# Where the zero fills of the sorted edge rows are issued in stage 1 of a graph network kernel

## The reference

```
def sage(x, W_l, b_l, W_r):
    agg = segment_sum(x[src], dst) / max(count(dst), 1)
    return agg @ W_l + b_l + x @ W_r
h = relu(sage(x, W_l1, b_l1, W_r1))
h = relu(sage(h, W_l2, b_l2, W_r2))
x = layernorm(x + h @ W_out + b_out)
# second network, per edge and then per node; row = src, col = dst
e = selu(concat(x[row], edge_attr) @ W1a + b1a) @ W1b + b1b
m = segment_sum(e, col) / max(count(col), 1)
y = selu(concat(x, m, u) @ W2a + b2a) @ W2b + b2b
out = layernorm(x + y)
```

## Time and profile before

| what | value |
|---|---|
| median of 3 runs | 2623.2 us (2621.38 to 2623.36) |
| the profiled execution's own time | 2619.25 us |
| its span | 2617.5 us |
| PE busy | 2105.8 us, 80% of the span |
| POOL busy | 1825.9 us, 70% |
| DVE busy | 1550.0 us, 59% |
| ACT busy | 987.8 us, 38% |
| fills of `sorted_edges` | 11 transfers of 1716 KB from SP's queue |

### The profile page before, as it was taken

The page is one execution under the profiler, slowest core; times in us unless marked ns, Lnnn a source line. Parts: engine busy times, 40 slices in busy tenths (PEclk is TensorE's granted clock), DMA queues, the critical chain, the costliest instruction groups (busy, mean ns, idle before and its releaser), DMA issues. The chain is left out here.

```text
span 2617.5 us, 52040 instructions
## 1 busy us (share of the span) xinstructions
PE 2105.8 (80%) x18382; PEld 1548.8 (59%) x18382; DVE 1550.0 (59%) x3098; ACT 987.8 (38%) x2255; POOL 1825.9 (70%) x1853
## 2 busy tenths in 40 slices
PE   1899999999999999847778787777787877866753
PEld 1555555555555555536666666666666666666753
DVE  6889999994455555545555555555555555543433
ACT  3777777771000000033333333333333333332322
POOL 5536766645766777677777777777777777777775
PEclk9989999999999999957898888988979889886555
DMA  8375787788677878334333333333333333322212
GB/s 293 126 230 191 208 257 225 202 250 227 231 231 226 240 232 239 86 103 115 74 72 69 72 68 68 75 68 71 74 63 78 72 62 79 68 61 51 54 40 45
DMA packets 478493, 346.45 MB, mean 132 GB/s; under 512 B 358165, under 2 KB 429008, under 8 KB 474574
## 3 DMA queue, kind: packets, MB, share of 16 engines
q1 hardware_dynamic: 367763, 272.49, 36.6%
q0 software_dynamic: 54240, 57.23, 9.9%
q10 hardware_dynamic: 56250, 13.52, 2.6%
HBM read 200.58 MB, written 142.39 MB: 131 GB/s over the span
## 5 line engine op out<-in xcount | busy, mean ns | idle before, releaser
L985 POOL DMA_INDIRECT A_sb<-source_terms,src_cur x1172 | 1120.3, 956 | 357.4 <-issue 351.6
L936 POOL DMA_INDIRECT sorted_edges<-pm_row,pm_to x440 | 482.2, 1096 | 171.1 <-issue 122.0
L1866 DVE TENSOR_TENSOR arena<-iota_code,arena 128x2048 f16<-128x2048 f16 (+1 forms) x392 | 438.5, 1188 | 33.7 <-PE cnt_ps L1413 31.3
L1080 ACT ACTIVATE A_sb<-cnt_ps 128x392 f32 (+1 forms) x784 | 384.1, 499 | 126.5 <-PE cnt_ps L1413 83.9
L1542 PE MATMUL agg_ps<-A_sb,arena 128*128 128x448 f16 x1911 | 375.5, 353 | 0.0
L2183 DVE TENSOR_TENSOR cnt_ps<-cnt_ps,A_sb 128x512 f32<-128x512 f32 x147 | 102.1, 695 | 459.3 <-DMA A_sb<-source_terms,src_cur 454.1
L1642 PE MATMUL agg_ps<-A_sb 128*65 128x48 f32 x2344 | 195.5, 245 | 181.4 <-DVE A_sb L2196 181.4
L1226 ACT ACTIVATE A_sb<-cnt_ps 128x512 f32<-128x512 f32 x147 | 87.6, 596 | 671.0 <-DVE cnt_ps L2183 665.7
L1413 PEld LDWEIGHTS cnt_ps<-arena 128*128 128x128 f16 x3136 | 190.2, 100 | 214.4 <-issue 168.8
L1413 PE MATMUL cnt_ps<-arena 128*128 128x98 f16 x3136 | 281.0, 214 | 31.3 <-ACT A_sb L1080 26.1
L1642 PEld LDWEIGHTS agg_ps<-A_sb 128*65 128x65 f32 x2344 | 181.2, 160 | 203.8 <-DVE A_sb L2196 198.6
(11 more groups left out here) (308 smaller groups left out, 3311.7 us busy)
## 6 DMA issues: line engine op xcount, KB each, us to landing
counts_matrix<-A_sb SPq DMA_DIRECT2D x14, 5488.0 KB, 17.4
A_sb<-counts_matrix SPq DMA_DIRECT2D x12, 5488.0 KB, 18.4
arena<-in_edge_attr_dram SPq DMA_DIRECT2D x96, 256.0 KB, 2.8
sorted_edges<-zrow SPq DMA_DIRECT2D x11, 1716.0 KB
A_sb<-source_terms,src_cur POOLq DMA_INDIRECT x1172
arena<-sorted_edges SPq DMA_DIRECT2D x143, 128.0 KB
overlapping_rows<-A_sb SPq DMA_DIRECT2D x1, 13056.0 KB, 39.3
A_sb<-in_edge_attr_dram SPq DMA_DIRECT2D x50, 256.0 KB, 2.8
```

The lines of the kernel that those rows point to most:

```text
L936: pool.indirect_dma_start(out=sorted_d, out_offset=bass.IndirectOffsetOnAxis(ap=pm_to[:, k, j:j + 1], axis=0), in_=pm_row[:, k, j, :], in_ ...
L985: pool.indirect_dma_start(out=gath[k][:, j * F:(j + 1) * F], out_offset=None, in_=p_d, in_offset=bass.IndirectOffsetOnAxis(ap=src_cur[k][: ...
L1080: act.activation(Asb(half)[:, :, bass.ds((b * BG + k) * GROUP, GROUP)].rearrange("p b (w j) -> p b w j", j=PAIR), cnt_ps[k % 2][:, 0:SUB * ...
L1866: ins = dve.tensor_tensor(hot_rows[:, slots], iota_code[:, 0:n, :].unsqueeze(1).to_broadcast([P, AT_ONCE * SUB // 2, n, 2]), turned[:, bas ...
```

## The change

Fills 0 to 10 are all issued inside `superblock(s)`, one per superblock from s = 2 to 12, behind the loads of group s-2 and ahead of the wait for the superblock's counts. Before, fills 0 and 1 were issued together between superblocks 1 and 2, and fills 2 to 10 behind the counts' stores of superblocks 4 to 12. The wait for scatter(0) stays ahead of fill 2 and moves with it. POOL's waits for the fills are not changed.

```diff
@@ -603,6 +603,10 @@
                 if s >= 2:
                     store_h(s - 2, half)
                     load_group(s - 2)
+                    if s == FIRST_SORT + 1:
+                        sp.wait_ge(pm_gone[0], 16 * EJ)
+                    if s - 2 < NR:
+                        blank(s - 2)
                 if s == NSB - 1:
                     for q in range(s - 1, IN_STAGE1 + PRING):
                         load_group(q)
@@ -619,15 +623,8 @@
                 sp.dma_start(pm_dst[:, :], dst[0:PG * EG].rearrange("(r q) -> r q", q=RG * EG)[:, 0].partition_broadcast(P)).then_inc(pm_dst_in, 16)
             superblock(0, 0)
             superblock(1, 1)
-            for r in range(2):
-                blank(r)
             for s in range(2, NSB):
                 superblock(s, s % 2)
-                if s >= FIRST_SORT + 1:
-                    if s == FIRST_SORT + 1:
-                        sp.wait_ge(pm_gone[0], 16 * EJ)
-                    if s - FIRST_SORT + 1 < NR:
-                        blank(s - FIRST_SORT + 1)
             sp.wait_ge(xT_ready, NSB - 2)
 
             def last_rows(rows, done):
```

## The result

The changed kernel takes 2613.15 us in the median of 8 runs (2611.82 to 2616.91), the kernel before 2621.51 us over 8 runs (2615.19 to 2623.85). The ratio is 0.9974 with a 95% interval of 0.9963 to 0.9985: 0.26% faster (the two medians alone lie 8.4 us, 0.32%, apart). Forecast were 2614.9 us and 0.32%. The profiled execution's span went from 2617.5 to 2611.2 us, 6.3 us less.

What follows compares the result with a forecast made beforehand. PE was taken to pace stage 1, losing time to a wait for x's rows held up by two fills, and its clock. -8.3 + 0 + 0 + 0 from 2623.2 gave 2614.9 us; range 2611.5 to 2620.5.

Steps and rivals of the forecast that it cites:

- The wait and its clock: Superblock 2, stage 1: PE's 2.93 us wait for x's rows and the clock's fall behind it go, gaining 8.3 us.
- The bottom-up sum: Superblock 2: 2.93 us of PE's wait plus 5.07 us of lowered clock make 8.0 us.
- rival 2: Superblock 2: only the wait goes, the clock's fall not coming from it; 2.9 us gained, 2620.3 us; chance 6%.
- Fills 2 to 10: SP's queue, superblocks 4 to 12: moving them from behind the counts' store to behind the group's load costs 0.
- The scatter beside a fill: POOL's scatter(s-3) issued beside a fill: no row; from below 0 to 8 us per superblock, taken as 0.
- One reading: A fill issued behind the load of 241.02 us would land by 252, when the counts' store comes.
- POOL's wait for fill 1: Before scatter(0): fill 1 lands 14 us behind the split's end, so POOL waits; cost to the kernel 0.
- Its cover: POOL's idle 5.40 us before the gather and 3.12 before the split absorb lateness; group 2's load keeps 4.8 us to spare.
- rival 4: POOL's wait for fill 1 makes group 2's load late for DVE and reaches PE: slower, 2632.0 us; chance 4%.
- Stages 2 and 3 ... should move forward by the 8.3 us: Stages 2 and 3 wait only for what comes from stage 1, so all move forward by 8.3 us.
- rival 1: Gain partly given back: a clock dip at the hand-over costs or gives 3 to 5 us; about 2619 us; chance 12%.
- One of the named signs of being wrong: Stage 1: the forecast is wrong if superblocks 4 to 12 grow past 38.9 us.

Runs made afterwards that it cites:

- The runs with more transfers: Changed kernel with one or two more fill-sized transfers to unread rows ahead of fill 1: ratios 1.0001 and 1.0003, on a third chip 1.0011 and 1.0040.
- the kernel with the early fills: As the changed kernel, but fills 0 and 1 go out ahead of superblock 0: 2618.87 us, ratio 0.9984 to the kernel before.
- the first and the fourth experiment: First: kernel before with only fills 0 and 1 moved, 2611.93 us; fourth: kernel before with a third fill-sized transfer ahead of x's rows, 2632.06 us.
- the second experiment: Kernel before with only fills 2 to 10 moved ahead of the counts' stores: 2620.58 us, ratio 0.9987.

## Why the prediction was right

**The wait and its clock (the 8.3 us).** Right in place and in size: 8.29 us by the stores of superblocks 2 and 3. The bottom-up sum was 2.93 + 5.07, the third fill's run measures 5.2 for the clock by itself, the run with fills 2 to 10 moved 6.3. That the clock's fall came from the wait (against rival 2) is shown: without the wait it is not there in three kernels (the changed one, the one with the first two fills moved, the one with them early), with a wait of 2.9 us or more it is there, in three kernels. A wait of 1.2 us did not bring it.

**Fills 2 to 10 (0 us).** Right: moved alone they make 0.9987 with 1 inside the interval. The scatter beside a fill, for which I had no row, is issued as fast as before (1.72 us at 241.73 us in the changed kernel, fill 2 having gone out at 239.35). One reading was off without cost: fill 2 was to have landed when the counts' store comes. Group 2's load was late and the superblock's end was not, so the store came 5.7 us behind the fill, and held SP for 1.50 us.

**POOL's wait for fill 1 (14 us, cost 0).** It is 16.0 us. The fill was issued at 196.15 and the scatter freed at 207.81, 11.7 us against my 10.3 (2 us of older traffic, 8.3 of fill). Its cover held in the way the prediction said: 5.4 and 3.1 us of idle time on POOL were used up, the rest passed on and was gone a superblock later. The cost was 0 where before takes some 2620 us. So the 14 us, feared as exposed in the prediction, were exposed on POOL and did not reach PE. I had tied rival 4 to one path, a late load of group 2 for DVE. The runs with more transfers show that path at 4.5 and 6.4 us of wait, but on the slow chips also a loss with hardly any wait of DVE, which I didn't see and whose cause stays open.

**The rest of the way.** "Stages 2 and 3 ... should move forward by the 8.3 us" is the weak step: the profile's span gained 6.3 and the ratio says 6.8 us (3.9 to 9.7). That looks like rival 1 in small: a superblock of stage 2 that takes 33.0 to 38.3 us from profile to profile, with the granted clock down to 0.80 in it before and to 0.71 after. The forecast's 2614.9 and the measured 2613.15 us lie closer than the two gains do, since the later runs of before came out lower as well; that part is luck. One of the named signs of being wrong also came: superblock 9 took 40.12 us, over the limit of 38.9. The limit was too tight, as before's own superblock 7 takes 39.38 us; the others from 4 to 12 stay at 38.85 or less.

## What to carry to other kernels

A wait of 3 us in front of the matrix engine cost 8, one of 1.2 us cost about itself: look for the granted clock behind each wait, and count both. A transfer that nobody waits for yet belongs behind the loads that somebody does, but well ahead of its own waiter: the wait that was covered on one chip came with a longer superblock on two others, though the cause there is not shown. The place in which no engine waits (one fill ahead of x's rows, one behind group 0's load) was the only one with an undisturbed superblock 4 on the slow chips (its superblock 2 took 42.18 us in one of the two profiles), though it was not timed where before takes 2620 us, and on the slow chips it is not told from before.

## What the runs showed of the hardware that was not expected

- The same program takes 2622, 3343 and 3384 us on three chips, with nearly equal busy times of POOL (1826 us in before's profile, 1802 to 1824 us in those of the slow chips). The idle time in front of the 1172 gathers is 357 us on the one and 936 us on the slowest, most of it without a named releaser.
- The clock's fall cost 5.4, 6.3 and 5.2 us after waits of 2.9, 3.2 and 11.6 us. After a wait of 1.2 us it did not come.
- It also falls where PE has waited for nothing long: superblock 9 of the changed kernel took 40.12 us (400.24 to 440.36) at a mean granted clock of 0.96, and in the kernel with the early fills one took 41.17 us, at 0.50 from 486 to 490. Superblocks of 40 us and more come at other places in the profiles of the first and the fourth experiment (41.07 and 41.32 us), and apart from those with PE's wait not at all in before's and the second experiment's. They may be a part of the scatter of some 4 us between runs; that was not tried.
- SP was held for 9.6 us by two fills with nothing ahead of them, and for 20.3 us with a counts' store ahead. Behind one counts' store and one fill even the small load of x's rows (112 KB) held it for 19.76 us; the same load behind a counts' store alone held it for 0.43 us. The instruction that is held can so be a small one, and whatever SP has behind it waits too.
